# A fused token, attention and FFN kernel on one core: FFN row statistics moved into the attention stage, and the FFN stage's order remade

## The reference, cut to what matters

```python
h = concat([tokens(x), text(x_txt)], axis=1)          # (64, 228, 192)
h = h + attention(layernorm(h, eps=1e-5))             # 12 heads of 16, k = v = q, causal
h = h + ffn(layernorm(h, eps=1e-5))

def rmsnorm(x, g):   return x * rsqrt(mean(x * x) + 1e-6) * g
def act_quant(x):    s = 127 / clip(max(|x|), 1e-5); return clip(round(x * s), -128, 127) / s
def bitlinear(x, w, g): return act_quant(rmsnorm(x, g)) @ weight_quant(w).T
def ffn(x):          return bitlinear(gelu(bitlinear(x, w1, g1)), w2, g2)   # 192 -> 768 -> 192
```

## Time and profile before

| | us |
|---|---|
| median of 3 runs (lowest, highest) | 1758.22 (1755.66, 1758.87) |
| the profiled execution | 1756.77 |
| its span, first to last instruction | 1755.0 |
| attention stage, with the start | up to about 1228 |
| FFN stage | from about 1228 on |
| TensorE busy in the span | 1474.0 (84%) |
| VectorE busy | 1460.8 (83%) |
| ScalarE busy | 1232.5 (70%) |
| GpSimd busy | 1099.7 (63%) |

### The profile page before, as it was taken

One profiled execution on the slowest core, in us unless ns is written; L12 is line 12 of the kernel. 1 busy time (PEld: TensorE's weight loads), 2 busy tenths in 40 slices (PEclk: granted clock), 3 DMA queues, 4 the chain that ended last, 5 costly groups with the idle time before them and its releaser, 6 DMA issues.

```text
span 1755.0 us, 53767 instructions
## 1 busy us (share of the span) xinstructions
PE 1474.0 (84%) x18602; PEld 1203.9 (69%) x18602; DVE 1460.8 (83%) x3227; ACT 1232.5 (70%) x1862; POOL 1099.7 (63%) x1369
## 2 busy tenths in 40 slices
PE   4799999999999999999999999985555565656565
PEld 2678888888888888888888888874444454545454
DVE  5578888888888888888888888864899999999996
ACT  0466676767667676767667676752788888888887
POOL 5456566666666665656665656541777777777775
PEclk8899999999999999999999999996677878777876
DMA  8533434333434342434343333310000000000000
GB/s 204 81 60 61 67 60 68 60 68 60 68 58 69 56 71 54 73 53 74 53 72 56 71 56 70 58 56 18 9 24 20 24 20 24 20 24 20 24 20 29
DMA packets 104194, 93.57 MB, mean 53 GB/s; under 512 B 22737, under 2 KB 94466, under 8 KB 104162
## 3 DMA queue, kind: packets, MB, share of 16 engines
q1 hardware_dynamic: 103394, 91.58, 27.5%
q0 software_dynamic: 768, 1.57, 0.4%
HBM read 74.12 MB, written 11.91 MB: 49 GB/s over the span
## 4 chain that ended last, share of the span: by engine, by line
PE 65%; DVE 19%; issue 7%; ACT 3%; POOL 1%; DMA 1%; DVEq 1%; SPq 1%; ACTq 0%; POOLq 0%
PE ps L1038 19%; PE ps L1095 9%; PE ps L1181 8%; DVE nmax L677 6%; PE ps L1172 5%; PE ps L1128 5%; DVE ff_st L814 4%; PE ps L1280 3%; PE ps L1160 3%; PE ps L1154 3%; PE ps L1261 3%; PE ps L1133 2%; PE ps L1076 2%; PE ps L1109 2%; DVE xpix L807 1%
## 5 line engine op out<-in xcount | busy, mean ns | idle before, releaser
L1038 PE MATMUL ps<-w_eff,pix 124*112 124x193 f32 (+1 forms) x2048 | 406.8, 337 | 11.6 <-DMA pix<-side 9.2
L677 DVE TENSOR_REDUCE nmax<-ps 116x12 bf16<-116x1344 f32 (+2 forms) x192 | 302.9, 1578 | 88.4 <-PE ps L1133 87.8
L493 POOL TENSOR_TENSOR pix<-probs,g_b 112x192 f32<-112x192 f32 (+1 forms) x512 | 298.4, 613 | 104.7 <-ACT probs L993 95.4
L881 ACT ACTIVATE probs<-ps,isw 116x688 f32<-116x688 f32 x384 | 299.1, 831 | 85.4 <-PE ps L1160 83.1
L1038 PEld LDWEIGHTS ps<-w_eff,pix 124*112 124x112 f32 (+1 forms) x2048 | 308.1, 166 | 38.3 <-issue 23.3
L420 POOL TENSOR_TENSOR xsq<-xsq 124x784 f32<-124x784 f32 (+1 forms) x128 | 184.3, 1440 | 218.1 <-ACT xsq L874 213.1
L440 POOL TENSOR_SCALAR_AFFINE_SELECT probs<-probs 116x464 f32<-116x464 f32 x384 | 274.1, 726 | 68.0 <-ACT probs L881 59.5
L863 ACT ACTIVATE pix<-xpix 54x896 f32<-54x896 f32 (+1 forms) x128 | 196.6, 1538 | 1.9 <-DMA xpix<-in_x 1.1
L1250 PE MATMUL ps<-ident_h,xpix 112*96 112x112 f16 (+1 forms) x256 | 34.9, 281 | 186.4 <-DVE xpix L831 186.4
L1095 PE MATMUL ps<-xnT,wq_pad 97*128 97x228 f32 (+1 forms) x768 | 166.5, 366 | 0.0
L1250 PEld LDWEIGHTS ps<-ident_h,xpix 112*96 112x96 f16 (+1 forms) x256 | 23.8, 167 | 197.8 <-DVE xpix L831 102.5
(11 more groups left out here) (134 smaller groups left out, 3230.9 us busy)
## 6 DMA issues: line engine op xcount, KB each, us to landing
xpix<-in_x SPq DMA_DIRECT2D x192, 196.0 KB
rden<-den_rows SPq DMA_DIRECT2D x256, 85.5 KB, 2.2
out<-xpix SPq DMA_DIRECT2D x64, 87.0 KB
out<-xpix SPq DMA_DIRECT2D x64, 84.0 KB
xpix<-in_x SPq DMA_DIRECT2D x128, 34.1 KB
h_all<-shift_w SPq DMA_DIRECT2D x5, 768.0 KB, 4.4
pix<-side SPq DMA_DIRECT2D x64, 36.8 KB
pix<-side SPq DMA_DIRECT2D x64, 36.6 KB
```

Of the source, the lines that this page charges most:

```text
L493: last = nc.gpsimd.tensor_tensor(v2[0:P, b, tile, cols], gel[0:P, b, tile, cols], g2_b[0:P, cols], ALU.mult)
L677: V.tensor_reduce(dst, src, AX_X, ALU.max, negate=True).then_inc(s_mx, 1)
L881: A(probs[0:TB, g, 2 * e:2 * e + 2, :], ps[0:TB, 4 + 2 * e:6 + 2 * e, 0:SK], ACT.Exp, scale=isw[0:TB, 7:8]).then_inc(s_p, 1)
L1038: last = MM(ps_tok[tile][0:P, :], pix[0:HI, par, o, lo:lo + P], w_eff[0:HI, o, :], start=(o == 0), stop=(o == OFFS - 1))
```

## The change

Row statistics of the FFN are taken in the attention stage: VectorE takes them for image n-1 in its step n, between maxima 0 and maxima 1 (`measure_rows`), and keeps the means in `mean2`; GpSimd takes the inverse roots of image n-2 in its step n, between the patch roots and the first masking (`row_roots`), and keeps them in `roots`. In the FFN stage, VectorE begins a step with the centring of m and its maximum, then takes the mean square of j, its maximum and only then the last addition of o; the product with the weight step moves behind the quantising of m and gets a semaphore of its own, for which GELU waits. GpSimd's power is on the two columns of j alone. ScalarE's order becomes quantising of j, copy of the first turn of m, copy of the second turn of j, GELU of m, squares of m. TensorE's becomes first turn of m, second turn of j, first products of m, second products of j; these are one step earlier than before, and still wait until the last addition of the image before them has been made (`f_y`, line 1277). Declarations of semaphores, the changed flags at the ends of the loops and the numbers of setup steps (two more memsets) are left out here.

```diff
@@ gpsimd
+            def row_roots(m):
+                pool.wait_ge(s_agg2, m + 1)
+                after(pool, s_rms, m)
+                apart(pool)
+                nc.gpsimd.tensor_scalar(ln_st[:, 32:34], ln_st[:, 35:38:2], 1.0 + EPS_RMS, EPS_LN * EPS_RMS,
+                                        ALU.mult, ALU.add).then_inc(s_var2, 1)
+                pool.wait_ge(s_var2, m + 1)
+                nc.gpsimd.tensor_tensor(roots[:, bass.ds(m * 4, 2)], ln_st[:, 32:34], expo[:, 0:2],
+                                        ALU.pow).then_inc(s_rms, 1)
...
                 if newer:
                     patch_roots(n + 2)
+                if prev:
+                    row_roots(n - 2)
                 if old:
                     clear_later(n, 0)
...
-                if new or mid:
-                    pool.wait_ge(f_var, i + 2)
-                    nc.gpsimd.tensor_tensor(ff_st[:, b, 20:24], ff_st[:, b, 16:20], expo[:, 0:4],
+                if mid:
+                    pool.wait_ge(f_var, i)
+                    nc.gpsimd.tensor_tensor(roots[:, bass.ds(i * 4 + 6, 2)], ff_st[:, b, 18:20], expo[:, 0:2],
                                             ALU.pow).then_inc(f_r1, 1)
@@ vector
+            def measure_rows(n):
+
+                dve.wait_ge(s_h2, n + 1)
+                apart(dve)
+                for tile, P in enumerate((TA, TB)):
+                    last = V.bn_stats(ln_st[0:P, 20 + 6 * tile:26 + 6 * tile], h_all[0:P, hcols(n, tile)])
+                last.then_inc(s_rowst, 1)
+                dve.wait_ge(s_rowst, n + 1)
+                after(dve, s_var2, n)
+                apart(dve)
+                for tile, P in enumerate((TA, TB)):
+                    last = V.bn_aggr(ln_st[0:P, 34 + 2 * tile:36 + 2 * tile], ln_st[0:P, 20 + 6 * tile:26 + 6 * tile])
+                last.then_inc(s_agg2, 1)
+                dve.wait_ge(s_agg2, n + 1)
+                V.tensor_copy(mean2[:, bass.ds(n * 2, 2)], ln_st[:, 34:38:2]).then_inc(s_mean2, 1)
...
                     maxima(n + 1, 0)
+                if prev:
+                    measure_rows(n - 1)
+                if new:
                     maxima(n + 1, 1)
@@ vector, ffn_step
                 if new:
-                    apart(dve)
-                    for tile, P in enumerate((TA, TB)):
-                        ins = V.bn_stats(st[0:P, 6 * tile:6 * tile + 6], h_all[0:P, hcols(m, tile)])
-                    flink(ins)
-                    apart(dve)
-                    for tile, P in enumerate((TA, TB)):
-                        ins = V.bn_aggr(st[0:P, 12 + 2 * tile:14 + 2 * tile], st[0:P, 6 * tile:6 * tile + 6])
-                    flink(ins)
-
-
-                    ins = V.tensor_scalar(st[:, 16:18], st[:, 13:16:2], 1.0 + EPS_RMS, EPS_LN * EPS_RMS,
-                                          ALU.mult, ALU.add)
-                if mid:
-                    dve.wait_ge(f_ssq, 2 * j + 2)
-                    ins = V.tensor_scalar(st[:, 18:20], gel_sum[:, 1 - b, :], 1.0 / HIDDEN, EPS_RMS, ALU.mult,
-                                          ALU.add)
-                if new or mid:
-                    ins.then_inc(f_var, 1)
-                if new:
+                    after(dve, f_q1, m)
                     for tile, P in enumerate((TA, TB)):
                         ins = V.scalar_tensor_tensor(v1[0:P, tile, :], h_all[0:P, hcols(m, tile)],
-                                                     st[0:P, 12 + 2 * tile:13 + 2 * tile], g1_b[0:P, :],
+                                                     mean2[0:P, bass.ds(m * 2 + tile, 1)], g1_b[0:P, :],
...
+                if mid:
+                    dve.wait_ge(f_ssq, 2 * j + 2)
+                    V.tensor_scalar(st[:, 18:20], gel_sum[:, 1 - b, :], 1.0 / HIDDEN, EPS_RMS, ALU.mult,
+                                    ALU.add).then_inc(f_var, 1)
+                if mid:
+                    dve.wait_ge(f_v2, 2 * j + 2)
...
                 if last_:
                     o = i - 3
                     dve.wait_ge(f_m2, o + 1)
...
-                    flink(V.tensor_tensor(st[:, 28:32], st[:, 20:24], st[:, 24:28], ALU.mult))
+                    flink(V.tensor_tensor(st[:, 28:32], roots[:, bass.ds(i * 4 + 4, 4)], st[:, 24:28], ALU.mult))
                     flink(V.tensor_scalar(st[:, 28:32], st[:, 28:32], 1e-5, None, ALU.max))
                     flink(V.reciprocal(st[:, 32:36], st[:, 28:32]))
-                    V.tensor_tensor(st[:, 40:44], st[:, 28:32], w_step[:, :], ALU.mult)
...
                     ins.then_inc(f_q1, 1)
+                if new or mid:
+                    V.tensor_tensor(st[:, 40:44], st[:, 28:32], w_step[:, :], ALU.mult).then_inc(f_step, 1)
@@ scalar, ffn_step
+                if mid:
+                    quantise(i, b, 0)
+                    quantise(i, b, 1)
                 if new:
                     act.wait_ge(f_t1, m + 1)
...
                 if mid:
-                    quantise(i, b, 0)
-                    quantise(i, b, 1)
-                if new:
-                    after(act, f_v2, 2 * m - 2)
-                    for tile, P in enumerate((TA, TB)):
-                        act.wait_ge(f_m1, 2 * m + tile + 1)
-                        A(gel[0:P, 1 - b, tile, :].rearrange("p (c d) -> p c d", c=2),
-                          ps[0:P, 2 + 2 * tile:4 + 2 * tile, 0:HIDDEN // 2], ACT.Gelu,
-                          scale=ff_st[0:P, b, 40 + tile:41 + tile]).then_inc(f_g, 1)
-                if mid:
                     act.wait_ge(f_t2, j + 1)
...
                     ins.then_inc(f_t2s, 1)
+                if new:
+                    after(act, f_v2, 2 * m - 2)
+                    act.wait_ge(f_step, m + 1)
+                    for tile, P in enumerate((TA, TB)):
+                        act.wait_ge(f_m1, 2 * m + tile + 1)
+                        A(gel[0:P, 1 - b, tile, :].rearrange("p (c d) -> p c d", c=2),
+                          ps[0:P, 2 + 2 * tile:4 + 2 * tile, 0:HIDDEN // 2], ACT.Gelu,
+                          scale=ff_st[0:P, b, 40 + tile:41 + tile]).then_inc(f_g, 1)
@@ tensor, ffn_step
                 if new:
                     turn_first(i + 1)
-                if last_:
-                    ffn_second(i - 2)
+                if mid:
+                    turn_second(i - 1)
                 if new:
                     ffn_first(i + 1)
                 if mid:
-                    turn_second(i - 1)
+                    ffn_second(i - 1)
```

More of the change, by code:

```diff
@@ L42 @@
 EPS_LN, EPS_RMS = 1e-5, 1e-6
-LIMIT, ROWB, TEXT, V_SETUP = 19, 26, 29, 33
+LIMIT, ROWB, TEXT, V_SETUP = 21, 28, 31, 35
 EARLY = 4
@@ L91, in build @@
         front_st = sb("front_st", [128, 16])
-        ln_st = sb("ln_st", [128, 32])
+        ln_st = sb("ln_st", [128, 40])
+        mean2 = sb("mean2", [128, IMAGES * 2])
+        roots = sb("roots", [128, (IMAGES + 2) * 4])
         tok_t = sb("tok_t", [128, 2, DIM])
@@ L230, in build @@
         s_h2 = sem("attention_added")
+        s_rowst = sem("row_statistics_ready")
+        s_mean2 = sem("row_means_kept")
+        s_agg2 = sem("row_variances_ready")
+        s_var2 = sem("row_mean_squares_ready")
+        s_rms = sem("row_roots_ready")
         f_var = sem("mean_squares_ready")
@@ L475, in _, with ffn_step @@
             step_images(IMAGES - 1, 0, None, newer=False, newest=False)
-            def ffn_step(i, b, new=True, mid=True):
-                if new or mid:
-                    pool.wait_ge(f_var, i + 2)
-                    nc.gpsimd.tensor_tensor(ff_st[:, b, 20:24], ff_st[:, b, 16:20], expo[:, 0:4],
+            row_roots(IMAGES - 2)
+            row_roots(IMAGES - 1)
+            def ffn_step(i, b, mid=True):
+                if mid:
+                    pool.wait_ge(f_var, i)
+                    nc.gpsimd.tensor_tensor(roots[:, bass.ds(i * 4 + 6, 2)], ff_st[:, b, 18:20], expo[:, 0:2],
                                             ALU.pow).then_inc(f_r1, 1)
@@ L506, in _ @@
             ffn_step(IMAGES - 2, 0)
-            ffn_step(IMAGES - 1, 1, new=False)
-            ffn_step(IMAGES, 0, new=False)
+            ffn_step(IMAGES - 1, 1)
+            ffn_step(IMAGES, 0)
         @block.vector
@@ L527, in _ @@
             step(V.memset(ff_st[:, :, :], 1.0))
+            step(V.memset(mean2[:, :], 1.0))
+            step(V.memset(roots[:, :], 1.0))
             step(V.memset(gel_sum[:, :, :], 1.0))
@@ L801, in ffn_step @@
                                               apply_absolute_value=True)
+                if mid:
[5 more added lines that the diff above has]
+                    for tile, P in enumerate((TA, TB)):
+                        ins = V.tensor_reduce(st[0:P, 26 + tile:27 + tile], v2[0:P, 1 - b, tile, :], AX_X,
+                                              ALU.max, apply_absolute_value=True)
+                if new or mid:
+                    flinks[0] += 1
+                    ins.then_inc(f_vc, 1)
                 if last_:
@@ L833, in ffn_step @@
                     ins.then_inc(f_q1, 1)
+                if new or mid:
```

(12 more changed lines are left out.)

32 lines of the change are left out of this document (15 added, 17 removed).

## The result

| | before | after |
|---|---|---|
| median of 4 runs (lowest, highest) | 1758.06 (1755.66, 1758.87) | 1774.88 (1772.98, 1775.92) |
| the profiled execution, its span | 1756.77, 1755.0 | 1774.59, 1772.9 |
| attention step, mean | 17.66 | 18.00 |
| FFN step, mean, from quantising to quantising | 7.96 | 7.86 |
| first quantising of the FFN stage starts at | 1247.14 | 1269.36 |

The ratio of after to before is 1.0097, with a 95% interval of 1.0085 to 1.011: slower by 1.0%, where 0.9% was forecast. The loss comes before the FFN stage: the first quantising is 22.2 us later (1269.36 − 1247.14). From the first to the last it takes 493.15 instead of 496.67, 3.5 less, and the tail is 0.8 shorter: 22.2 − 3.5 − 0.8 = 17.9, the difference of the spans.

The account below looks back on a forecast made before the run. TensorE was taken to bound the attention stage, VectorE the FFN stage. Attention 25.4, passage +1 and FFN −11 gave +15 us, 1772 for the profiled execution and 1773 for the median; range 1736 to 1793.

Parts of the forecast that it names:

- The attention stage: VectorE's row statistics, 1.21 us in a 0.80 us gap, delay TensorE 0.41 us in each of 62 steps: +25.4 us.
- the passage between the stages: Between attention and FFN stages, the last rows need statistics and roots after the last addition: +1 us (−1 to +2).
- GpSimd's row roots: In the attention stage, a small operation and a power ahead of the first masking: 1.3 us together, costed at nothing.
- The cover: Margin by which GpSimd's masking of the second group still ends before the value products need it: 0.1 us.
- VectorE in the FFN stage: 1.61 us of work goes per image, so VectorE's own work falls from about 7.95 to 6.3 us a step.
- ScalarE's loop: In the FFN stage, ScalarE's new order takes 7.13 us a step at the high clock, 8.38 at the low.
- The clock: TensorE's clock in the FFN stage keeps its mixed pattern, thirds at 7.13, 7.8 and 8.38 us; mean step 7.77.
- the 11 us that the FFN stage was to give: FFN saving from a step of 7.77 instead of 7.95 us, over 62 steps: −11 us.
- The high clock: Rival: shorter TensorE pauses keep the FFN clock at 2.4 GHz, step 7.13 us, total 1734 to 1744; chance 0.22.
- The cheap insertion: Rival: overlaps cut the attention delay to 0.15 us a step, 9 us in all; total 1757; chance 0.11.
- GpSimd on the path: Rival: in the attention stage GpSimd's masking comes late for the value products, 19 us more, 1792; chance 0.10.
- a low clock throughout: Rival: every FFN step at the low clock, 8.38 us, costs 27 us in that stage, 1811; chance 0.05.

Follow-up runs that it names:

- split kernel: The kernel after with only the two statistics left between first and second maxima, aggregation and copy of means moved behind the inversion; 1749.45 us, ratio 0.9958.
- filled kernel: The kernel after with 14 unused matmuls of 240 columns per FFN step and a TensorE wait for GELU added; 1741.99 us, ratio 0.9901.
- fastest kernel: The split kernel with ScalarE's and TensorE's FFN orders of before and 14 unused matmuls behind the second turn of each step; 1699.74 us, ratio 0.9676.
- squares in the gap: The split kernel with ScalarE's squares of the image before between its two copies and VectorE's mean square behind the GELU maxima; 1765.17 us, ratio 1.0039.

## Why the prediction was right, and where it was not

**The attention stage** carried the forecast and was right in kind and nearly in size. The gap of 0.80 us and the insertion of 1.20 gave a shift of 0.40 between the two maxima, and TensorE's wait of 0.43. But the step grew by 0.34. The split kernel, whose second maxima are as early as before, shows where the missing part lies: its step is 17.59, 0.07 shorter than before. So something of the edit shortens the step by 0.07, and 0.41 − 0.07 = 0.34. No run was made on it, but the traces show where the 0.07 lies. From 540 to 960 us of the kernel before, the value products start 0.59 us after the start of the last scores (L1154) in the three steps that last 17.59, and 0.64 or 0.69 after it in the others; in these others VectorE's last subtraction of the queries (L666, for which they wait too, line 1169) ended only 0.15 us ahead of them. In the split kernel and in the kernel after it ends 0.66 us ahead, and all value products start at 0.59. Before, then after:

```profile
899.90 1.44 DVE L638 SCALAR_TENSOR_TENSOR h_all<-tok_t,front_st,bw 112x192 f32 x2
902.22 0.86 DVE L666 TENSOR_TENSOR q_lo<-ps,q_hi 128x684 f16<-128x684 f32 x1
```

```profile
898.99 0.86 DVE L690 TENSOR_TENSOR q_lo<-ps,q_hi 128x684 f16<-128x684 f32 x1
900.51 1.38 PE L1208 MATMUL ps<-probs,vaug 112*32 112x228 f32 x32
...
915.23 0.74 DVE L662 SCALAR_TENSOR_TENSOR h_all<-tok_t,front_st,bw 112x192 f32 x2
```

The two operations that VectorE does ahead of its queries (L638, L662 after) take 1.44 us beside GpSimd's first maskings (from 899.32) and 0.74 where the row roots have pushed these back to 916.48. That the roots on GpSimd so gave back the 0.07 is read from the traces and was not tested alone. Together with the passage between the stages the forecast was 26.4, and 22.2 came.

**GpSimd's row roots** were undersized at 1.3 us and still cost nothing. GpSimd in one step after:

```profile
914.75 0.62 POOL L445 TENSOR_SCALAR ln_st<-ln_st 128x2 f32<-128x2 f32 x1
915.57 0.95 POOL L448 TENSOR_TENSOR roots<-ln_st,expo 128x2 f32 x1 [0.19 <-POOL ln_st L445]
916.48 2.26 POOL L458 TENSOR_SCALAR_AFFINE_SELECT probs<-probs 116x464 f32<-116x464 f32 x4
```

From 914.75 to 916.48 are 1.73 us. The cover that I had put at 0.1 us was thicker: the four maskings then run in one go, 2.26 us instead of 1.81 and 1.32 with 0.47 idle between them, so what the roots take in front comes back behind, and no wait of TensorE for GpSimd stands among those of the stage.

**VectorE in the FFN stage** falls to 334.79 / 400 × 7.86 = 6.6 us a step, not 6.3. The 6.3 took the whole step of 7.95 us for work, though VectorE was busy only 370.50 / 400 × 7.96 = 7.4 of it; less the 1.5 us of work that went, 5.9 would be left. The operations left there grew: centring takes 538 ns on the average (407 in the kernel before, same shape) and the weight step 546 (359), and in the timeline both now stand beside GpSimd's weighing. So the term was 0.3 us too small, and would have been 0.7 too small without the waits in it; it had no effect, since VectorE waits for GpSimd (55.7 us above).

**ScalarE's loop** was right step by step at each level of the clock: 7.13 forecast and 7.09 to 7.41 measured in the fast steps, 8.38 forecast and 8.0 to 8.3 in the slow ones. The copy of the second turn was to start 2.66 or 3.20 us after quantising; in the steps above it starts 2.61 and 3.23 after.

**The clock** is the step that failed: "I take the same pattern: a third at 7.13, a third at 8.38, and a third between". 38 of 62 steps are at 8.0 or more, the granted clock is 0.67 against the 0.75 to 0.8 named, and the mean step 7.86 against 7.77. TensorE's long pause was not cut into three of 1 to 1.5 us either: the one ahead of the second turn is 1.9 us in the mean and up to 3.0, and only two shorter ones of up to 1.3 stand beside it in a part of the steps. Of the 11 us that the FFN stage was to give, 4 came. This error of 7 us and that of the attention stage, 4 us the other way, cancel to 2.5 us; that the time was met within 2 is luck to that extent.

The sentence "Before, the same low clock cost little, because VectorE closed the loop" is not borne out: a clock of 0.89 instead of 0.79 was worth 0.28 us a step before, one of 0.96 instead of 0.67 was worth 0.53 after. Yet executions of the kernel before with mean granted clocks of 0.88 and 0.91 took the same time (1756.95 and 1756.81 us), so the mean clock alone does not price a step, and which instructions have to run low to cost time was not found. Its picture of the kernel before was incomplete as well. VectorE stood in the loop, but through its order more than through its load: taking 1.6 us off it gave nothing, reordering it gave 0.29, and only behind that was the load worth 0.27. A VectorE busy for 93% of the stage looked full; the statistics in it had only filled its wait for ScalarE's squares.

**The rivals.** The high clock (1734 to 1744) did not occur in the change; the filled kernel, at 0.96, gave 1741.99. Its price was right, and its condition not met. The cheap insertion, GpSimd on the path and a low clock throughout did not occur either.

## What to carry to other kernels

Measure a gap against the whole insertion with its waits before work is moved into it: 0.80 us of idle time took 0.6 us of statistics for nothing and not 1.21, and the rest belonged at a second place. A high share of busy time doesn't say that an engine's load bounds a loop; take the load off in one kernel and change its order in another, and see which moves the step. Where two engines hand one image to and fro, place other work between the two halves, or each slowing of the one is paid in full by the other.

## What was not expected of the hardware

TensorE's granted clock did not follow the length of its longest waits. The kernel after had shorter ones than the kernel before (1.9 us in the mean, 3.0 at most, against 2.9 and 4.0) and a lower clock, 0.67 against 0.78. The fastest kernel kept waits of 1.7 us in the mean and up to 2.5, at 0.96; the kernel with the squares in the gap had none over 2.2 us, and 0.59, the lowest clock. The main wait of TensorE in the kernel before (1310 to 1710 us), in the fastest, and in that with the squares in the gap (1300 to 1660 us), then the stretches of the last two:

```profile
PE ps L1250 <- DVE xpix L831: 145.9, 50, 4.0
```

```profile
PE ps L1291 <- DVE xpix L867: 84.7, 49, 2.5
```

```profile
PE ps L1291 <- DVE xpix L867: 47.1, 45, 1.8
PE ps L1321 <- DVE xpix L849: 24.3, 45, 2.2
```

```profile
1300.00:1660.00 360.00, 267.46 (x2538) 217.39 (x2537) 348.81 (x813) 339.50 (x608) 288.97 (x456) 0.96 0.08 25
```

```profile
1300.00:1660.00 360.00, 271.70 (x1607) 202.66 (x1608) 313.63 (x715) 299.18 (x535) 253.73 (x404) 0.59 0.07 22
```

The first did 2538 matmuls and the second 1607, in the same 360 us. But the number does not order the kernels either: before and after did 1814 and 1836 in 400 us, at 0.78 and 0.67. What the grant follows stays open. The Trainium skill, page "TensorE: Matmul & The Clock Gate", section "HAM oscillation — how this bites in real kernels", blames the oscillation on long pauses. By that rule alone the change would have kept the clock up, and the squares in the gap all the more; these rows do not agree. Matmuls that nobody needs did raise it in three kernels, and each became faster (by 33, 18 and 17 us); their own cost was not measured apart.

Some small operations on VectorE are priced by their neighbour: the same 128x4 operation (L853) took 0.17 us with GpSimd idle and 0.52 while it weighed. From 1300 to 1700 us it took 0.17 in all 19 cases beside an idle GpSimd, and 0.45 to 0.58 in 25 of 26 beside a busy one. The reciprocal of the same shape behind it took 0.18 in every case. VectorE in the kernel after, with GpSimd's weighing beginning at 1534.55 and at 1542.16:

```profile
1534.02 0.17 DVE L853 TENSOR_SCALAR ff_st<-ff_st 128x4 f32<-128x4 f32 x1
...
1542.82 0.52 DVE L853 TENSOR_SCALAR ff_st<-ff_st 128x4 f32<-128x4 f32 x1
1543.37 0.18 DVE L854 RECIPROCAL ff_st<-ff_st 128x4 f32<-128x4 f32 x1
```
